# Four of twelve context chunks weighed by products of halves in a decoder layer with cross-attention

## The reference, cut to what matters

```
q = (Q @ WQ).reshape(N, ql, HEADS, DK)          # 16 heads of 64
k = (K @ WK).reshape(N, kl, HEADS, DK)          # K = V = the context
v = (V @ WV).reshape(N, kl, HEADS, DV)
compat = einsum('nqhk,nlhk->nhql', q, k) / sqrt(DK)
weights = softmax(compat, axis=3)
attn = einsum('nhqk,nkhv->nqhv', weights, v).reshape(N, ql, HEADS * DV)
return attn @ WO + bO
```

## Time and profile before

| | before |
|---|---|
| median of 3 runs | 1574.97 us (1573.03 to 1577.52) |
| the profiled execution's own time | 1572.63 us |
| its span | 1570.9 us |
| TensorE busy | 96% of the span |
| VectorE, ScalarE, GpSimd busy | 72%, 58%, 50% |
| granted TensorE clock, mean | 0.99 of full speed |

### The profile page before, as it was taken

The page is one execution under the profiler, slowest core; times in us unless marked ns, Lnnn a source line. Parts: engine busy times, 40 slices in busy tenths (PEclk is TensorE's granted clock), DMA queues, the critical chain, the costliest instruction groups (busy, mean ns, idle before and its releaser), DMA issues.

```text
span 1570.9 us, 25257 instructions
## 1 busy us (share of the span) xinstructions
PE 1513.6 (96%) x7599; PEld 1091.9 (70%) x7599; DVE 1124.2 (72%) x1816; ACT 904.8 (58%) x1238; POOL 792.8 (50%) x407
## 2 busy tenths in 40 slices
PE   5897999999999999999999999999999999999897
PEld 3446767777777777777777777777777777777485
DVE  3338785868686868777786868686868686987756
ACT  4235675666666666666566666566666666665421
POOL 2002374555556565656555555555555556665611
PEclk9998998999999999999999999999999999999999
DMA  4100011100000000000001000100000000110000
GB/s 152 39 6 15 1 40 40 39 29 38 26 38 28 39 38 39 39 39 39 39 39 39 39 39 39 39 39 36 38 27 38 26 38 32 40 40 20 0 1 24
DMA packets 15251, 54.92 MB, mean 35 GB/s; under 512 B 1111, under 2 KB 6314, under 8 KB 15214
## 3 DMA queue, kind: packets, MB, share of 16 engines
q1 hardware_dynamic: 15214, 54.46, 9.2%
HBM read 53.54 MB, written 0.92 MB: 35 GB/s over the span
## 4 chain that ended last, share of the span: by engine, by line
PE 81%; DVE 9%; ACT 5%; issue 3%; POOL 1%; DMA 0%; DVEq 0%; POOLq 0%; ACTq 0%
PE ps L733 33%; PE ps L699 27%; PE ps L589 3%; PE ps L594 3%; PE ps L580 3%; DVE arena L1298 3%; PE ps L573 3%; PE ps L792 2%; ACT arena L990 2%; PE ps L713 2%; PE ps L511 1%; POOL arena L443 1%; ACT arena L890 1%; PE ps L721 1%; DVE arena L1284 1%
## 5 line engine op out<-in xcount | busy, mean ns | idle before, releaser
L1284 DVE TENSOR_TENSOR arena<-arena,ps 125x896 f32<-125x896 f32 x336 | 363.9, 1083 | 98.2 <-PE ps L699 98.0
L443 POOL TENSOR_TENSOR arena<-arena,ring 125x896 f32<-125x896 f32 x192 | 417.7, 2175 | 17.4
L699 PE MATMUL ps<-q_hi,ctxT_hi 128*125 128x448 f32 x768 | 400.5, 522 | 2.4 <-ACT arena L984 1.0
L443 POOL TENSOR_TENSOR arena<-arena 125x896 f32<-125x896 f32 x112 | 236.9, 2115 | 316.4 <-ACT arena L990 307.4
L733 PE MATMUL ps<-ring,ctx_nat 125*128 125x448 f32 x768 | 345.3, 546 | 0.0
L984 ACT ACTIVATE ring<-ps 125x896 f32<-125x896 f32 x192 | 176.3, 918 | 239.2 <-PE ps L733 148.9
L699 PE MATMUL ps<-q_hi,ctxT_lo 128*125 128x448 f32 x768 | 281.7, 367 | 0.0
L699 PE MATMUL ps<-q_lo,ctxT_hi 128*125 128x448 f32 x768 | 281.6, 367 | 0.0
L733 PE MATMUL ps<-arena,ctx_nat 125*128 125x448 f32 x576 | 242.9, 544 | 2.5
L1298 DVE TENSOR_TENSOR ring<-ring,ps 125x896 f32<-125x896 f32 x192 | 202.0, 1081 | 0.0
L699 PEld LDWEIGHTS ps<-q_hi,ctxT_hi 128*125 128x125 f32 x768 | 144.2, 188 | 64.2 <-issue 47.3
(11 more groups left out here) (204 smaller groups left out, 1923.8 us busy)
## 6 DMA issues: line engine op xcount, KB each, us to landing
ctx_raw<-in_ctx_dram SPq DMA_DIRECT2D x32, 750.0 KB
ctx_nat<-in_ctx_dram SPq DMA_DIRECT2D x32, 750.0 KB
w_sb<-in_L_ffn_W_dram SPq DMA_DIRECT2D x1, 1024.0 KB
resid<-in_x_dram SPq DMA_DIRECT2D x1, 896.0 KB, 6.5
out_dram<-ctx_raw SPq DMA_DIRECT2D x4, 224.0 KB, 2.5
ctx_raw<-in_L_xattn_WQ_dram SPq DMA_DIRECT2D x1, 512.0 KB
w_sb<-in_L_xattn_WK_dram SPq DMA_DIRECT2D x1, 512.0 KB
w_sb<-in_L_xattn_WV_dram SPq DMA_DIRECT2D x1, 512.0 KB
```

Of the source, the lines that this page charges most:

```text
L443: g.tensor_tensor(summed, chunk[0] if j == 1 else summed, chunk[j], ALU.add).then_inc(s["prob_added"], 1)
L699: m = mm(score_ps[j % 2][:, half, :], cx[k][:, rows], q[k][:, cols], start=(n == 0), stop=(n == 2))
L1284: v.tensor_tensor(run_max, kept(k, 0) if j == 1 else run_max, score_ps[j % 2], ALU.max).then_inc(s["maxed"], 1)
```

## The change

For pairs 0 to 13, chunks 5, 7, 9 and 11 are weighed by products of halves. ScalarE copies the exponentials of such a chunk into `p_hi` (type fp32r), GpSimd subtracts to get `p_lo`, and GpSimd makes `ctx_hi` and `ctx_lo` of these four context chunks once a period. TensorE multiplies hi by hi, lo by hi for each half of the columns, and then hi by lo for both, six fp32r products in the place of two float32 products. There is one `p_hi` and one `p_lo`, shared by the four chunks, and one pair of context halves. The sums (s) of k = 1 move from (9, 3), (10, 0), (10, 1), (10, 2) to (10, 1), (10, 2), (10, 3), (11, 0). `query_lo` of k = 0 moves from chunk 9 to chunk 10, and the last addition of the heads to the end of the period. To make room, some tiles now share their space with others, and the bias b1 is loaded late into the space of a context buffer.

```
+    SPLIT = (5, 7, 9, 11)
...
-        PLACES = (... , ".... .... .... .... .... .... t... t.q. t.q. q.qs sss. ....")
+        PLACES = (... , ".... .... .... .... .... .... t... t.q. t.q. q.q. .sss s...")
+        LOW_AFTER = {4: 5, 6: 7, 8: 9, 10: 11}
+            def halves_free(b, j):
+                n = SPLIT.index(j)
+                return CH * b + (SPLIT[n - 1] + 1 if n else 0)
...
+            def context_halves(i, k):
+                nb = 2 * i + k
+                chunks = slice(SPLIT[0], SPLIT[-1] + 1, SPLIT[1] - SPLIT[0])
+                need(pool, f"nat_in{k}", 16 * (i + 1))
+                need(pool, "weighted", CH * nb)
+                g.tensor_tensor(ctx_hi[:], ctx_nat[k][:, chunks, :], ones[...], ALU.mult).then_inc(s["ctx_hi_done"], 1)
+                need(pool, "ctx_hi_done", nb + 1)
+                g.tensor_tensor(ctx_lo[:], ctx_nat[k][:, chunks, :], ctx_hi[:].bitcast(F32), ALU.subtract).then_inc(s["ctx_lo_done"], 1)
+            def low_probability(b, k, j):
+                need(pool, "prob_hi_done", split_count(b, j))
+                g.tensor_tensor(p_lo[:], kept(k, j), p_hi[:].bitcast(F32), ALU.subtract).then_inc(s["prob_lo_done"], 1)
...     GpSimd's period: behind the add of chunk j
+                    if j in LOW_AFTER and LOW_AFTER[j] in split_chunks(i, k):
+                        low_probability(b, k, LOW_AFTER[j])
...     TensorE's weigh
+                if j in split_chunks(i, k):
+                    n = SPLIT.index(j)
+                    if half == 0:
+                        if n == 0:
+                            need(pe, "ctx_lo_done", b + 1)
+                        need(pe, "prob_hi_done", split_count(b, j))
+                    for cx in (ctx_hi, ctx_lo):
+                        mm(usum_ps[:, half, :], cx[:, n, :], p_hi[:, half, :], start=False, stop=False)
+                    if half == 1:
+                        need(pe, "prob_lo_done", split_count(b, j))
+                        for part in range(2):
+                            m = mm(usum_ps[:, part, :], ctx_hi[:, n, :], p_lo[:, part, :], start=False, stop=(j == CH - 1))
...     ScalarE
+            def high_probability(b, k, j):
+                need(act, "prob_done", step_count(b, j))
+                need(act, "weighted", halves_free(b, j))
+                a(p_hi[:], kept(k, j), ACT.Copy).then_inc(s["prob_hi_done"], 1)
...     its period
                 for j in range(CH):
+                    if j > SPLIT[0] and j + 1 in split_chunks(i, k):
+                        high_probability(b, k, j + 1)
...
+                    if j == SPLIT[0] - 2 and split_chunks(i, k):
+                        high_probability(b, k, SPLIT[0])
...     VectorE's period
-                    if j == (6 if k else 9) and not last_pair:
+                    if j == (6 if k else 10) and not last_pair:
                         query_lo(i + 1, k)
```

More of the change, by code:

```diff
@@ L68, in decoder_layer @@
         resid_k = resid[:].rearrange("p (k d) -> p k d", k=PAIRS)
-        xnorm = sb("xnorm", [TOK, PAIRS, D])
+        p_hi, p_lo = [sb(name, [CR, 2, HALF], F32R) for name in ("p_hi", "p_lo")]
+        ctx_hi, ctx_lo = [sb(name, [CR, NS, D], F32R) for name in ("ctx_hi", "ctx_lo")]
         xT = sb("xT", [D, PAIRS, TOK])
@@ L353, in _ @@
                     load_context(i, k)
+            need(sp, "ctxT_ps", MP * B)
+            sp.dma_start(b1_sb, b1).then_inc(s["b1_in"], 16)
             out_k = out.rearrange("b s d -> (b s) d").rearrange("(k p) d -> p k d", p=TOK)
@@ L730, in weigh @@
                         need(pe, f"nat_in{k}", 16 * (i + 1))
-                if half == 0 or j == 0:
-                    need(pe, "prob_done", step_count(b, j, half))
-                m = mm(usum_ps[:, half, :], ctx_nat[k][:, j, :], kept(k, j)[:, half, :], start=(j == 0), stop=(j == CH - 1))
+                if j in split_chunks(i, k):
[10 more added lines that the diff above has]
+                            m = mm(usum_ps[:, part, :], ctx_hi[:, n, :], p_lo[:, part, :], start=False, stop=(j == CH - 1))
+                else:
+                    if j == half == 0 and isinstance(i, int) and i == PAIRS - 2 and k == 0:
+                        need(pe, "ctx_lo_done", b + 1)
+                    if half == 0 or j == 0:
+                        need(pe, "prob_done", step_count(b, j, half))
+                    m = mm(usum_ps[:, half, :], ctx_nat[k][:, j, :], kept(k, j)[:, half, :], start=(j == 0), stop=(j == CH - 1))
                 if half == 1:
@@ L1076, in period @@
                     if j == 6 and isinstance(i, int) and i == PAIRS - 1 and k == 0:
-                        act.wait_ge(s["ffn_w_in"], 16 * 7)
-                        a(b1_r[0:E, 0, :], b1_sb[:], ACT.Copy).then_inc(s["b1_hi_done"], 1)
-                assert not slot_work(i, k, CH - 1) or last
+                        act.wait_ge(s["b1_in"], 16)
+                        a(b1_r[0:E, 0, :], b1_sb, ACT.Copy).then_inc(s["b1_hi_done"], 1)
+                assert last or all(what == "sums" for what, _, _ in slot_work(i, k, CH - 1))
             sequence(act, period)
@@ L1128, in scale @@
                 dve.wait_ge(s["rstd_done"], GROUPS * (count - 1) + q + 1)
+                if count == 3:
+                    need(dve, "xT_ps", 2 * GROUPS + q - 1 if q > 1 else 0)
                 for t in range(G4 * q, G4 * q + G4):
-                    m = v.tensor_scalar(xnorm[:, t, :], resid_k[:, t, :], meanvar[:, t, 0:1], rstd[:, t:t + 1], ALU.subtract, ALU.mult)
+                    m = v.tensor_scalar(normed(count, t), resid_k[:, t, :], meanvar[:, t, 0:1], rstd[:, t:t + 1], ALU.subtract, ALU.mult)
                 m.then_inc(s["ln_done"], 1)
@@ L1331, in add_heads, with finish_heads @@
                     m.then_inc(s["head_added"], 1)
-                if which == 3:
-                    need(dve, "head_added", H * (pair + 1))
-                    v.tensor_tensor(tile, tile, odd_heads[:], ALU.add).then_inc(s["x2_done"], 1)
+            def finish_heads(pair):
+                tile = resid[:, bass.ds(pair * D, D)]
+                need(dve, "head_added", H * (pair + 1))
+                v.tensor_tensor(tile, tile, odd_heads[:], ALU.add).then_inc(s["x2_done"], 1)
             route_count = [0]
@@ L1452, in period @@
                     side_reads(i, k, j, range(4))
+                if k == 0 and not (isinstance(i, int) and i == 0):
+                    finish_heads(i - 1)
             sequence(dve, period)
```

41 lines of the change are left out of this document (28 added, 13 removed).

## The result

| | before | after |
|---|---|---|
| median | 1574.97 us (1573.03 to 1577.52) | 1693.71 us (1676.94 to 1697.19, 5 runs) |
| profiled execution, its span | 1572.63, 1570.9 us | 1676.94, 1675.2 us |
| mean granted TensorE clock | 0.99 | 0.953 profiled, 0.942 to 0.944 in the other four |

The ratio is 1.0755 (95%: 1.0732 to 1.0778): slower, by 118.7 us by the medians and by 104.3 us from span to span. The prediction was 1623 us, with 1584 to 1648. The direction came true, the size did not. The profiled execution is the fastest of the five and has the highest clock of the five; what follows explains its 104.3 us.

What follows compares the result with a forecast made beforehand. TensorE, 96% busy, was taken as the bound. 14 x (2.9 longer in k = 1 less 0.6 shorter in k = 0) = 32 us, plus 16 for the clock, on 1575 gave 1623 us; range 1584 to 1648.

Steps and rivals of the forecast that it cites:

- The clock: Behind TensorE's wait in k = 1, clock falls to half in two of three periods, 1.7 us each: 16 us.
- the upper bound of 24: Clock loss if the fall behind the k = 1 wait came in every period: 24 us.
- without `weigh` of 10: k = 1, first sums to turned maximum: 5.67 us instead of 7.45, without that `weigh` and with a cheaper chunk 11.
- Rival 4: The clock falls in all 14 periods behind the k = 1 wait: 1631 us; chance 0.25.
- the fall of the earlier trace: End of before: half clock for 3.4 us behind a 3.07 us TensorE wait for GpSimd, 1.7 us lost.
- 0.28 us less a chunk: `weigh` on TensorE: six fp32r products take 1.22 us instead of 1.50, saving 1.12 us a period, 31.4 in all.
- time taken off TensorE is time gained: TensorE, busy 96% of the span, sets the time, as long as nothing it waits for comes later.
- 0.6 shorter: Period of k = 0: 1.12 us saved on TensorE, about 0.5 lost, so 0.6 us shorter.
- I take 0.5 lost: k = 0: `query_lo` beside low 11 costs VectorE or GpSimd up to 0.9 us; 0.5 taken.
- close, but hidden: k = 0: GpSimd's low halves end just before TensorE needs them, low 11 near 794.0 against 794.7.
- Rival 1: GpSimd's low halves are cheap, 1.12 us each: 1553 us, at the very best 1544; chance 0.10.
- some 6 us: How much smaller the sum would be if a low half took 1.97 us, the Trainium skill's scaled figure.

Runs made afterwards that it cites:

- the first experiment: Changed kernel with six unread float32 products of 256 columns filling TensorE's wait ahead of the first sums of k = 1: 1637.05 us, ratio 1.038.
- the second run: Changed kernel without GpSimd's low halves, TensorE multiplying by the high half again instead (low part missing from the result): 1577.12 us, ratio 1.002.
- ninth: Changed kernel with two float32 products of 256 columns ahead of each of the four pieces of sums in k = 1, wait kept: 1710.44 us, ratio 1.087.
- thirteenth: Changed kernel with six float32 products filling the wait and two more ahead of each piece of sums in k = 1: 1670.78 us, ratio 1.061.
- the seventh: Kernel without low halves, plus two float32 products of 256 columns ahead of each of the four pieces of sums in k = 1: 1598.2 us, ratio 1.016.
- third run: Changed kernel with all its moves, but every chunk weighed in float32 and no products of halves: 1572.05 us, ratio 0.999.
- The twelfth run: Changed kernel with only chunks 5 and 9 in halves, sums at their old places and `query_lo` of k = 0 back at chunk 9: 1570.35 us, ratio 0.998.

## Why the prediction was wrong, point by point

**The clock: the step that failed.** "I count the fall in two of three, a choice from one case of the same kind: 14 x 2/3 x 1.7 = 16 us." It fell in 14 of 14, for 6.8 or 10.2 us in thirteen and 13.7 in the first, not 3.4. By the price of a fall from the first experiment, 3.2 us (and 50.7 - 45.93 = 4.8 for the longer), the thirteen periods lost 7 x 3.2 + 6 x 4.8 = 51 us, and the upper bound of 24 that made the end of the range was half of that. I had seen that this stretch loses its float32 chunk (5.67 us "without `weigh` of 10") and booked that as a gain. It was the second cause: narrow work without a wait lowers the clock in most periods (10 of 13 in the second run, 7 of 13 in the first), the wait alone for 6.8 us in all (ninth), both together for 6.8 or more (the changed kernel), neither never (thirteenth). Rival 4 had the right count, one of the two causes and half the price. Why the fall of the earlier trace rows, behind the longest wait of all, lasted only 3.4 us is open.

"One case" was also not true of the trace of before. In its first pair it has another, in this very stretch of k = 1, which the prediction leaves out:

```profile
247.24 0.86 PE L580 MATMUL ps<-ones,arena 125*112 125x1 f32 x8
249.90 1.00 PE L580 MATMUL ps<-ones,arena 125*112 125x1 f32 x8 [0.95 <-ACT arena L968]
```

```profile
251.00:252.00 1.00, 1.00 (x2) 0.55 (x3) 0.12 (x1) 0.00 (x0) 0.00 (x0) 0.50 0.00 0
```

Between one-column sums TensorE waits for 0.95 us, the clock is at half from 250.7 on for 10.2 us, and the period takes 49.12 us where the others take 43.02: 5.1 us for the fall. With that price in all 14 pairs the forecast would have been 1575 + 32 + 71 = 1678 us, an estimate made with the result known.

The Trainium skill (TensorE: Matmul & The Clock Gate, HAM oscillation) speaks of gaps in TensorE's work that bring the lower clock in each round anew. The ninth run agrees, with 6.8 us each time; the second run shows a case beside it, a fall with no gap, which is gone in the seventh.

**What the products save: some chunks save nothing.** "0.28 us less a chunk", 1.12 a period, was 0.89 in k = 1 and 0.55 in k = 0. The second run against the third shows it chunk by chunk. Chunks 7 and 9 save 0.26 to 0.29 us in both periods, and chunk 11 saves 0.29 in k = 1, as forecast. Chunk 5 saves 0.06 and 0.00, and chunk 11 nothing in k = 0. For these TensorE is not the last to be ready, as in chunk 6 of k = 0, in before and in the changed kernel:

```profile
774.78 2.08 DVE L1298 TENSOR_TENSOR ring<-ring,ps 125x896 f32<-125x896 f32 x2
777.00 0.64 PE L573 MATMUL ps<-ident,ctx_raw 125*128 125x125 f32 x4
827.18 2.08 DVE L1373 TENSOR_TENSOR late_ring<-late_ring,ps 125x896 f32<-125x896 f32 x2
829.40 0.65 PE L621 MATMUL ps<-ident,ctx_raw 125*128 125x125 f32 x4
```

The first turned piece starts 0.14 us behind the end of VectorE's subtraction, 14.40 us into the period before and 14.41 after. In the same way, the turned maximum of k = 0 starts 0.13 us behind the end of VectorE's last maximum, in the second run as in the third. The prediction's "time taken off TensorE is time gained" looked for later work on GpSimd and ScalarE, and not on VectorE.

**k = 0: the gain was mis-sized, the loss was not.** "0.6 shorter" was 0.0 (39.66 against 39.62). The gain is the 0.55 above. The loss was forecast too: `query_lo`, "beside low 11: VectorE or GpSimd loses up to 0.9 ... I take 0.5 lost". In the changed kernel:

```profile
845.63 1.88 DVE L1348 TENSOR_TENSOR q_lo<-arena,q_hi 128x896 fp32r<-128x896 f32 x1
847.44 1.07 DVE L1359 TENSOR_TENSOR arena<-arena,ps 125x896 f32<-125x896 f32 x1
848.65 1.06 PE L761 MATMUL ps<-ident,arena 125*112 125x125 f32 x8 [0.61 <-DVE arena L1359]
```

Beside low 11 and the last add `query_lo` takes 1.88 us; without low halves it takes 1.08 at the same place. The last maximum comes later, and TensorE waits for it 0.6 us where it waits 0.12 without low halves. That is 0.5 of the 0.6 us between the two kernels (39.66 and 39.07). The twelfth run says nothing on this, as it has no low half beside `query_lo`; a run of the four-chunk kernel with `query_lo` at chunk 9 is missing. TensorE never waits for GpSimd in k = 0, so "close, but hidden" held.

**What held.** A low half takes 2.12 us; the chain of adds and low halves 34.1 us (34.2). The wait at chunk 7 was 0.70 us (0.9), that for the last add 2.48 (3.2). Without a fall, k = 1 is 45.93 - 43.02 = 2.9 us longer, as forecast. Its parts, by the first run against the second: 2.7 for the products in the wait's place, 1.1 around the wait at chunk 7, less 0.9; forecast were 3.2, 0.8 and 1.1. That the sum agrees to a tenth is luck. Bias and shared tiles cost nothing (third run), nor do the context halves, which the third run does not make: TensorE has no wait for them in the changed kernel. Rival 1 ("the low halves are cheap") is out by the 2117 ns of their group. Two small slips changed nothing: the "some 6 us" beside the estimate of 1.97 us would be 9 by the pitch of 2.19 (3 x 0.22 x 14), and the fall of the earlier trace rows stands from 1493.1 to 1496.5.

**The sum.** Per pair the forecast had 2.9 - 0.6 + 1.1 = 3.4; measured are 2.9 + 0.0 + 3.9 = 6.8. The clock is 2.8 of the 3.4 that were missing, k = 0 the other 0.6. The measured 3.9 for the clock rest on 45.93 us for the changed kernel without a fall, taken from the first experiment. The runs that were not profiled have a lower clock yet, 0.943 against 0.953, which would account for the 17 us between the profiled execution and the median (1% of 1675).

## What to carry to other kernels

Before taking wide products out of a stretch of TensorE's work, or moving narrow ones into it, read what is left there from first to last: the clock can fall without any wait, and the stretch that it falls in then takes up to twice as long. A wait of 2.5 us costs more in the clock behind it (3.1 us with wide work behind, 4.8 where a longer fall followed) than in itself. Look through the whole trace for stretches at half clock before you price a fall, the first round of the loop too.

Before booking a saving on the busiest engine, look at each place where it meets another: where the other is ready last, the saving is lost (chunk 5 here). And where a helper's chain (copy, subtract, add) runs through three engines, do the share of the change that keeps its last link off the critical place: two chunks in halves won 0.8% with the later sums and at most 0.2% with the old ones, three lost 2 to 7%, four lost 7.5%.

## What was not expected of the hardware

- The granted clock fell with TensorE busy in every microsecond and no wait before it: at 670 us in the second run, nearly 4 us after the first of the one-column products. All falls that I read in the loop lasted 3.4, 6.8, 10.2, 13.7 or 17.1 us.
- Products that compute nothing can pay, in the place of a wait: six of them made the changed kernel 57 us faster (1637.05 us). The eight among the one-column sums, 49 us of work, cost 34 us beside those six (1670.78) and 21 in the kernel without low halves: the steady clock paid part of them back and never all.
- `query_lo` on VectorE takes 1.88 us beside a low half and an add on GpSimd, and 1.08 without the low half; the add beside it takes 2.96 instead of 2.1.
- On GpSimd a subtraction of 125x896 with two different inputs takes 2.12 us, and with the same input twice 1.68.
